# Experts stage: logits as eight more columns of Wo's matmuls, denominators inverted in a 128-partition layout, two decision groups, bf16 one-hot matrices

## The chip, the cores and the metric

One core of a Trainium2 chip. The metric is the device time of the whole program in microseconds, the median of the runs shown; each profile is of one execution more.

## What is computed

Two transformer layers with modulation, for 2048 tokens of 512 features. Layer 0 is attention and then a top-1 mixture of eight experts; layer 1 is a state-space block and a small block-diagonal MLP. The change lies in layer 0's second half, called experts here:

```
x = x + ga * (softmax-weighted values / denominators) @ Wo.T     (the end of attention)
h = layernorm(x) * (1 + cb) + sb
logits = h @ gate_w.T + gate_b;  selected = argmax(logits)
x = x + gb * (h @ expert_w[selected].T + expert_b[selected])
```

## The kernel before

`experts()` (lines 807 to 1372) holds 16 tiles of 128 tokens (TT), four to a chunk of 512 columns (PER, NCH). One list of instructions per engine is written by hand, and semaphores alone order them. All that follows is in the order of those lists.

**Start.** Attention has left numerators (`scratch.num`, 64 rows of 2048) and denominators (`scratch.den`, 8 rows) in memory. SP loads the numerators, Wo, a turned Wo, small constants and then the eight expert matrices of 1 MB (lines 945 to 957). ACT issues two loads of the denominators, each row repeated for the eight values of its head, so that they lie like the numerators, 64x2048 (L1119). PE spreads the gates over all partitions as rows (L997), takes the mean of the gate weights (L1004), the contribution of the shift to the logits (L1009), the product of the centred gate weights with x (L1015, four chunks, 32 rows each for four feature blocks, summed later by a matrix called collect) and Wo times the gate weights (L1020). ACT copies the product to SBUF as `xw` (L1125). DVE multiplies Wo by the gate row (L1200), then for each chunk inverts the 64x512 denominators (L1209); it multiplies chunk 0 itself (L1212), GpSimd the other three (L975).

**Loop over 16 tiles.** PE: Wo's matmul of a tile, 512 columns (L1050), then two matmuls of 8 columns that give its logits, one with `xw` and collect, one with Wo times the gate weights (L1051, L1052). A matmul in f32 is two passes in the trace. Three banks take Wo's results (A_BANKS). DVE: the residual, x plus that bank (L1218), statistics (L1222, L1226) and the inverse deviation (L1232, L1234). ACT: the square root (L1129) and, two tiles at a time, the normalised h (L1133), which it stores by chunks (L1136). The logits aren't of the normalised h: since the layer norm is linear but for its mean and deviation, they are the product of x with centred weights, scaled later by the inverse deviation.

**Decisions.** For each chunk of four tiles, `decide` (L1247 to L1254, eight steps of DVE, each waits for the one before) scales the logits, finds the largest and writes a one-hot matrix, `onehot`. PE counts by matmuls with a triangle and a matrix of ones (L1036, L1038, L1039, all f32), and `put` (L1264 to L1274) turns the counts into each token's rank with its expert, the number of full tiles before it, its row in its tile, and a matrix `at_row`. Decisions 0 to 2 and placements 0 and 1 stand in the loop of DVE, between tiles; the rest comes after the last tile.

**Tail.** DVE works out how many tiles of 128 each expert fills (L1299 to L1303), each token's tile, and the matrices (L1307 to L1310) with which PE (L1064) finds the source token of every slot in 23 tiles (TILES). GpSimd then issues indirect loads of h by these sources (L981). From then on PE turns each tile (L1079), multiplies it with its expert's matrix (L1099), and in between adds the experts' biases in four groups of four tiles (L1085 before tile 0, L1071 after tiles 0, 1, 2), turned by the one-hot rows from L1060. After the last tile the results are gathered back (L989), added and normalised, and the state space begins.

Of the kernel before, what the change touches and what calls it, by code (L numbers as in the profile page):

```python
# [17 lines left out]
F32 = mybir.dt.float32  # L18
BF16 = mybir.dt.bfloat16
# [787 lines left out]
def experts(nc, d, g, scratch):  # L807
# [9 lines left out]
    A_BANKS = 3  # L817
# [4 lines left out]
    PICK = 8  # L822
    TEMPER = float((HEADS * E) ** -0.5)
    with ExitStack() as ctx:
        sb, sem = sb_alloc(ctx, nc), sem_alloc(ctx, nc, "moe")
        wo = sb("moe_wo", [AC, D])
        wos = wo
# [4 lines left out]
        wow = sb("moe_wo_logits", [AC, EXPERTS])  # L832
        collect = sb("moe_collect", [P, EXPERTS])
# [6 lines left out]
        order = sb("moe_order", [P, 2, P])  # L840
        iota = sb("moe_iota", [P, EXPERTS])
        filled = sb("moe_filled", [P, NCH + 1, EXPERTS])
# [22 lines left out]
        onehot = sb("moe_onehot", [P, TT, 32])  # L865
        whole = sb("moe_whole", [P, EXPERTS, TT])
# [9 lines left out]
        above = sb("moe_above", [P, TT, TT])  # L876
        full = sb("moe_full", [P, TT])
        within = sb("moe_within", [P, TT])
# [7 lines left out]
        xw = srt  # L886
# [3 lines left out]
        ps_rows = [psum[:, b, :] for b in (0, 1)]  # L890
        ps_a = [psum[:, b, :] for b in range(A_BANKS)]
        ps_x = [psum[:, b, :] for b in (4, 5, 6, 7)]
        ps_gate = [psum[:, b, 0:PER * EXPERTS].rearrange("p (t e) -> p t e", e=EXPERTS) for b in (4, 5, 6, 7)]
        ps_pos = psum[:, 3, 0:(PER + 1) * EXPERTS].rearrange("p (t e) -> p t e", e=EXPERTS)
        ps_source = psum[:, 2, 0:TILES * 2]
        ps_mean, ps_c, ps_wow = (psum[:, b, 0:EXPERTS] for b in (3, 2, 3))
        ps_turn = psum[:, 4, :].rearrange("p (n t) -> p n t", n=NCH)
# [4 lines left out]
        logit_in, wo_in, count_in, experts_in = (sem(n) for n in ("logit_in", "wo_in", "count_in", "experts_in"))  # L902
        att_in = [sem("att_first_in"), sem("att_rest_in")]
        rows_mm, rows_out, gated, pool_set, den_done, first_ready, rest_ready = (sem(n) for n in (
            "rows_mm rows_out gated pool_set den_done first_ready rest_ready").split())
        wg_step, setup_mm, setup_out, x_mm, xw_out = (sem(n) for n in "wg_step setup_mm setup_out x_mm xw_out".split())
        WG_SCALED, WG_CENTRED, WG_GATED = 1, 2, 3
        MEAN_MM, C_MM, WOW_MM = 1, 2, 3
        PAD_SET, ONES_SET, HOTS_SET = 1, 2, 3
        att_mm, x1_done, stat_done, var_done, sd_done, rstd_done, shift_done, h_done, gate_mm = (sem(n) for n in (  # L910
            "att_mm x1_done stat_done var_done sd_done rstd_done shift_done h_done gate_mm").split())
        empty_set, pick, chosen_done, pos_mm, pos_step, ranked, place_step, found = (sem(n) for n in (
            "empty_set pick chosen_done pos_mm pos_step ranked place_step found").split())
# [12 lines left out]
        COUNTS = ((order[:], "order"), (iota[:], "iota"), (across[:], "across"), (row[:], "row"), (starts[:], "starts"), (tiles[:], "tiles"))  # L926
# [15 lines left out]
        def _(sp):  # L942
            for b in range(2):
                part = slice(b * HALF, (b + 1) * HALF)
                sp.dma_start(att[0:HEADS * E, part], scratch.num[:, part]).then_inc(att_in[b], 16)
                if b == 0:
                    sp.dma_start(wo[:], d["wo"]).then_inc(wo_in, 16)
                    sp.dma_start(wot[:], d["wot"].rearrange("(k p) c -> p k c", p=P)).then_inc(wo_in, 16)
# [44 lines left out]
        def _(pe):  # L993
# [34 lines left out]
            def positions(i):  # L1028

                pe.wait_ge(chosen_done, i + 1)  # L1030
                if i >= 1:
                    pe.wait_ge(ranked, i)
# [1287 lines left out]
```

## Time and profile before

| | us |
|---|---|
| median of 3 runs | 1777.32 |
| lowest, highest | 1776.28, 1777.55 |
| the profiled execution | 1780.89 |
| its span in the trace | 1779.1 |
| experts, before the first gather | 498.56 to 583.07 |
| busy in the span: PE, DVE, ACT, POOL | 1490.2, 1322.9, 1134.0, 924.0 |
| mean granted clock of TensorE | 0.874 |

The span is the profiled execution without what lies around it. A busy share is an average over stages with different bounds, so the stage of the change is read by its own stretches and in order of time. The granted clock is in parts of 2.4 GHz: 0.50 is the level of 1.2 GHz, 1.00 that of 2.4 GHz. An idle time in brackets is that of the engine just before, with what ended it.

### The profile page before, as it was taken

The page shows a single profiled execution, that of the slowest core. Times are in us where ns is not written, and L with a number is a line of the kernel's source. Part 1 is how long each engine was busy: PE and PEld are TensorE (multiplying, and loading weights), DVE is VectorE, ACT ScalarE, POOL GpSimd, SP SyncE. Part 2 cuts the span into 40 slices and gives each one's busy share as a digit, 9 for nine tenths or more (in the row PEclk, how much of TensorE's full clock was granted, in tenths as well). Part 3 has the DMA queues.
Part 4 walks back from the last instruction along what each step waited for, and adds up shares of the span by engine and source line. Part 5 has one row for each costly group of instructions (what it writes and reads, how often), then busy time and mean ns, then how long its engine had stood idle before and what let it go on. Part 6 is the DMA issues. An engine that isn't in the chain of part 4 may idle for free. (4 is left out here: it accounts for less than half of the span.)

```text
span 1779.1 us, 26522 instructions
## 1 busy us (share of the span) xinstructions
PE 1490.2 (84%) x9052; PEld 815.1 (46%) x9052; DVE 1322.9 (74%) x2126; ACT 1134.0 (64%) x2277; POOL 924.0 (52%) x603
## 2 busy tenths in 40 slices
PE   5888999999978895678688898998989888755668
PEld 2441222222246443556365575665657566422432
DVE  3339999999056414107999999999999999999232
ACT  2323777777922233347788878878887887855138
POOL 0000000001010223326999999999999999999303
PEclk9875999999965897699799899999999999866689
DMA  6411112221072345823354554555554554644112
GB/s 247 160 43 42 28 32 81 79 81 59 3 231 95 101 137 206 290 69 87 96 137 114 132 136 118 129 122 118 135 130 119 125 125 108 137 101 112 68 51 95
DMA packets 154386, 199.10 MB, mean 112 GB/s; under 512 B 17567, under 2 KB 124999, under 8 KB 152716
## 3 DMA queue, kind: packets, MB, share of 16 engines
q1 hardware_dynamic: 142252, 163.81, 34.3%
q0 software_dynamic: 5168, 18.63, 3.2%
q10 hardware_dynamic: 6832, 14.96, 2.3%
q8 instruction: 72, 1.18, 0.3%
q14 instruction: 62, 0.51, 0.1%
HBM read 151.08 MB, written 46.28 MB: 111 GB/s over the span
## 5 line engine op out<-in xcount | busy, mean ns | idle before, releaser
L2040 DVE TENSOR_TENSOR_SCAN shared<-ssm_psum,ssm_state,shared 128x256 f32<-128x256 f32 x1024 | 674.9, 722 | 20.7 <-ACT ssm_state L1927 12.2
L1940 ACT ACTIVATE ssm_psum<-shared,ssm_a 128x256 f32<-128x256 f32 x1024 | 443.6, 468 | 157.7 <-DVE shared L2040 151.3
L1662 POOL TENSOR_TENSOR shared<-shared,ssm_bc 128x1024 f32<-128x1024 f32 x256 | 509.3, 2000 | 35.4 <-DVE shared L2040 16.0
L734 ACT ACTIVATE att_probs<-att_psum 128x1024 f32<-128x1024 f32 x256 | 248.3, 1021 | 75.2 <-PE att_psum L661 72.6
L1639 POOL TENSOR_TENSOR shared<-shared,ssm_bc 128x1024 f32<-128x1024 f32 x144 | 287.9, 1999 | 12.2 <-DMA shared<-drive_rows 12.2
L775 DVE TENSOR_REDUCE att_rowmax<-att_psum 128x1 f32<-128x512 f32 x448 | 277.5, 681 | 3.3 <-PE att_psum L634 1.5
L1765 PE MATMUL ssm_psum<-shared,ssm_select 128*32 128x256 f32 x2048 | 170.4, 423 | 93.9 <-POOL shared L1662 93.3
L603 POOL COPY att_v<-v_tokens 128x128 f32<-128x128 f32 x8 | 2.3, 292 | 298.8 <-ACT att_out L728 298.8
L634 PE MATMUL att_psum<-att_k,att_q 32*128 32x512 bf16 x448 | 138.0, 398 | 9.9 <-DVE att_rowmax L775 7.3
L1700 PE MATMUL ssm_psum<-ssm_h,late_weights 128*128 128x256 f32 x512 | 133.0, 421 | 9.3 <-ACT shared L1900 5.4
L673 PE MATMUL att_psum<-att_probs,att_v 128*32 128x512 f32 x1024 | 137.2, 608 | 0.6 <-ACT att_probs L734 0.6
L661 PE MATMUL att_psum<-att_q,att_k 32*128 32x512 bf16 (+2 forms) x1344 | 136.7, 385 | 0.0
L2025 DVE TENSOR_TENSOR shared<-shared,ssm_psum 128x1024 f32<-128x1024 f32 x112 | 133.4, 1191 | 3.6 <-DMA shared<-drive_rows 3.6
L1751 PE MATMUL ssm_psum<-shared,late_weights 128*128 128x256 f32 x512 | 123.3, 396 | 7.9 <-ACT ssm_xout L1913 7.3
L1765 PEld LDWEIGHTS ssm_psum<-shared,ssm_select 128*32 128x32 f32 x2048 | 46.7, 112 | 180.0 <-POOL shared L1662 100.9
L1700 PEld LDWEIGHTS ssm_psum<-ssm_h,late_weights 128*128 128x128 f32 x512 | 107.0, 213 | 37.5 <-issue 13.1
L1743 PE MATMUL ssm_psum<-ssm_h,late_weights 128*128 128x256 f32 x512 | 123.6, 397 | 0.0
L1709 PE MATMUL ssm_psum<-ssm_upre,late_weights 128*128 128x256 f32 x512 | 117.2, 381 | 0.6 <-ACT late_turned L1846 0.5
L1751 PEld LDWEIGHTS ssm_psum<-shared,late_weights 128*128 128x128 f32 x512 | 99.2, 198 | 30.9 <-ACT ssm_xout L1913 9.7
L1743 PEld LDWEIGHTS ssm_psum<-ssm_h,late_weights 128*128 128x128 f32 x512 | 99.4, 198 | 23.0 <-issue 8.9
L1709 PEld LDWEIGHTS ssm_psum<-ssm_upre,late_weights 128*128 128x128 f32 x512 | 95.6, 189 | 19.8 <-issue 4.5
L661 PEld LDWEIGHTS att_psum<-att_q,att_k 18*128 18x128 bf16 (+2 forms) x1344 | 47.1, 93 | 115.5 <-ACT att_probs L734 89.8
(261 smaller groups left out, 1822.3 us busy)
## 6 DMA issues: line engine op xcount, KB each, us to landing
shared<-drive_rows SPq DMA_DIRECT2D x256, 256.0 KB, 4.5
qkv_wmod<-in_wmod SPq DMA_DIRECT2D x8, 1536.0 KB, 12.3
shared<-in_x SPq DMA_DIRECT2D x8, 1024.0 KB, 5.1
late_weights<-in_we SPq DMA_DIRECT2D x8, 1024.0 KB, 13.4
ssm_bc<-bc_rows SPq DMA_DIRECT2D x32, 256.0 KB, 5.2
drive_rows<-ssm_delta SPq DMA_DIRECT2D x64, 128.0 KB, 1.7
drive_rows<-ssm_du SPq DMA_DIRECT2D x64, 128.0 KB, 1.8
sorted_results<-moe_y ACTq DMA_DIRECT2D x23, 256.0 KB, 2.0
```

The lines of the kernel that those rows point to most:

```text
L661: last = nc.tensor.matmul(ps_s[half][:, j, :], kst[rows, s, a // 2, kt * P:(kt + 1) * P], qst[rows, s, a, :], start=(a == 0), stop=(a == P ...
L734: nc.scalar.activation(probs[:, u % RING, :].rearrange("p (j t) -> p j t", j=2), ps_s[u % 2], ACT.Exp).then_inc(exp_done, 1)
L775: nc.vector.tensor_reduce(rowmax[:, at:at + 1], ps_m[n % MB], AX.X, ALU.max).then_inc(max_done, 1)
L1639: nc.gpsimd.tensor_tensor(drive(Q), rep[:, s % 2, 1], bc[:, c % 2, 0, gr, :].unsqueeze(1).to_broadcast([P, J, SW]), ALU.mult).then_inc(poo ...
L1662: nc.gpsimd.tensor_tensor(read(Q), drive(Q), bc[:, c % 2, 1, gr, :].unsqueeze(1).to_broadcast([P, J, SW]), ALU.mult).then_inc(read_done, 1)
L1700: last = nc.tensor.matmul(halves("proj", c, pair)[:, i], win[:, k, m:m + P], h[:, c % 2, k, :], start=(k == 0), stop=(k == KT - 1))
L1709: last = nc.tensor.matmul(halves("conv", c, pair)[:, i], conv[:, 2 * pair + i, k, :], upre[:, pair % 2, i, k:k + SW], start=(k == 0), stop ...
L1743: last = nc.tensor.matmul(halves("gate", c, pair)[:, i], win[:, k, m:m + P], h[:, c % 2, k, :], start=(k == 0), stop=(k == KT - 1))
L1751: nc.tensor.matmul(bank("out", c, m)[:, 0:SW], wout[:, t, m * P:(m + 1) * P], gate[:, c % 2, t, :], start=(t == 0), stop=False)
L1765: last = nc.tensor.matmul(ps_y[t % 2][32 * j:32 * j + 32, :], select[:], read(Q)[:, j, :], start=(gr == 0), stop=False)
L1940: nc.scalar.activation(ps_decay[n % HALF_BANKS][:, i], rep[:, s % 2, 0, j, :], ACT.Exp, scale=amat[:, t, gr, j:j + 1]).then_inc(decay_done, 1)
L2040: nc.vector.tensor_tensor_scan(drive(Q)[:, j, :], ps_decay[(2 * Q + j // 2) % HALF_BANKS][:, j % 2], drive(Q)[:, j, :], state[:, t, gr, j: ...
```

## The change

The logits no longer have matmuls of their own. `att`, the left operand of Wo's matmul, grows from 65 to 104 rows: rows 96 to 103 hold the product of x with the centred gate weights (summed over the features by PE, copied by ACT and brought there by four DMAs from SP), rows 65 to 95 are zero. Wo grows by eight columns, which hold Wo times the gate weights and, in rows 96 to 103, an identity. The 520 columns are computed as two matmuls of 260 in two neighbouring banks; three such pairs replace the three banks. ACT copies the eight logit columns to SBUF and gives the pair free together with DVE.

The denominators are loaded once as 128 partitions x (8 heads x 16 tokens), inverted there, stored to memory and only then loaded repeated. DVE multiplies all four chunks, three of them in its loop. There are two groups of decisions, 12 tiles and 4; the first stands in the loop after tile 14's statistics, both placements after the loop. One-hot, triangle, ones and the identity that turns the one-hot rows are bf16. The number of full tiles comes from one addition that rounds to a multiple of 128 by a large constant instead of a comparison and a sum. The spreading of GATE_B, its copy and the bias product (now GpSimd's) move behind the loop; the first bias group moves behind tile 0. SP's expert weights come behind the four DMAs, which wait for the copy.

```diff
-    A_BANKS = 3
+    AR = 96 + EXPERTS
+    WIDE = D + EXPERTS
+    CUT = WIDE // 2
+    A_SLOTS = 3
+    GROUPS = ((0, 12), (12, TT))
+    TO_TILES = 3.0 * float(P << 22)
-        order = sb("moe_order", [P, 2, P])
+        order = sb("moe_order", [P, 2, P], BF16)
+        identity = sb("moe_identity", [P, P], BF16)
-        att = sb("moe_att", [AC, T])
+        att = sb("moe_att", [AR, T])
+        sums = sb("moe_sums", [P, HEADS, T // P])
-        onehot = sb("moe_onehot", [P, TT, 32])
+        onehot = sb("moe_onehot", [P, TT, 32], BF16)
+        ps_a = [flat[:, 2 * s * W + W - CUT:2 * s * W + W - CUT + WIDE] for s in range(A_SLOTS)]
```

On SP, behind the constants:

```diff
+            sp.wait_ge(xw_out, 1)
+            sp.wait_ge(pool_set, ONES_SET)
+            for i in range(NCH):
+                sp.dma_start(att[AR - EXPERTS:AR, i * W:(i + 1) * W], xw[32 * i:32 * i + EXPERTS, :]).then_inc(xw_in, 16)
+            sp.dma_start(be[:], d["be"]).then_inc(be_in, 16)
```

On GpSimd:

```diff
+            nc.gpsimd.memset(att[HEADS * E:AR - EXPERTS, :], 0.0).then_inc(pool_set, 1)
-            for i in range(1, NCH):
-                sl = slice(i * W, (i + 1) * W)
-                pool.wait_ge(den_done, i + 1)
-                nc.gpsimd.tensor_tensor(att[0:HEADS * E, sl], att[0:HEADS * E, sl], den[0:HEADS * E, sl], ALU.mult).then_inc(rest_ready, 1)
+            pool.wait_ge(rows_out, len(ROW))
+            pool.wait_ge(be_in, 16)
+            nc.gpsimd.tensor_tensor(bes[:], be[:], rows[:, ROW[GATE_B]], ALU.mult).then_inc(pool_set, 1)
```

On PE:

```diff
+            for k in range(KT):
+                for i in range(NCH):
+                    last = nc.tensor.matmul(ps_x[32 * i:32 * (i + 1), :], wc[:, k, :], xt[:, k, i * W:(i + 1) * W], start=(k == 0), stop=(k == KT - 1))
+            last.then_inc(setup_mm, 1)
+            pe.wait_ge(gated, 2)
+            pe.wait_ge(xw_in, 16 * NCH)
...
             for n in range(TT):
+                if n % PER == 0:
+                    pe.wait_ge(att_ready, n // PER + 1)
+                if n >= A_SLOTS:
+                    pe.wait_ge(x1_done, n - A_SLOTS + 1)
+                    pe.wait_ge(gate_out, n - A_SLOTS + 1)
-                nc.tensor.matmul(ps_a[n % A_BANKS], att[:, n * P:(n + 1) * P], wos[:], start=True, stop=True).then_inc(att_mm, 1)
-                nc.tensor.matmul(ps_gate[n // PER][:, n % PER, :], xw[:, n // PER, n % PER * P:(n % PER + 1) * P], collect[:], start=True, stop=False)
-                nc.tensor.matmul(ps_gate[n // PER][:, n % PER, :], att[:, n * P:(n + 1) * P], wow[:], start=False, stop=True).then_inc(gate_mm, 1)
+                a = ps_a[n % A_SLOTS]
+                nc.tensor.matmul(a[:, 0:CUT], att[:, n * P:(n + 1) * P], wo[:, 0:CUT], start=True, stop=True)
+                nc.tensor.matmul(a[:, CUT:WIDE], att[:, n * P:(n + 1) * P], wo[:, CUT:WIDE], start=True, stop=True).then_inc(att_mm, 1)
+                if n == 2:
+                    for k in range(KT):
+                        last = nc.tensor.matmul(ps_c, g.mod[:, 0, SHIFT_B, k:k + 1].to_broadcast([P, P]), wg[:, k, :], start=(k == 0), stop=(k == KT - 1))
+                    last.then_inc(setup_mm, 1)
+            positions(0)
+            pe.wait_ge(x1_done, TT)
+            pe.wait_ge(gate_out, TT)
+            spread_row(1, GATE_B)
+            positions(1)
```

On ACT:

```diff
+            act.dma_start(sums[:], scratch.den.rearrange("h (p b) -> p h b", p=P)).then_inc(sums_in, 16)
+            act.wait_ge(rows_mm, 1)
+            nc.scalar.copy(rows[:, 0], ps_rows[0]).then_inc(rows_out, 1)
+            act.wait_ge(sums_done, 1)
+            act.dma_start(scratch.rec.rearrange("h (p b) -> p h b", p=P), sums[:]).then_inc(sums_out, 16)
+            act.wait_ge(sums_out, 16)
-                act.dma_start(den[0:HEADS * E, part], scratch.den[:, part].unsqueeze(1).to_broadcast([HEADS, E, HALF])).then_inc(att_in[b], 16)
+                act.dma_start(den[0:HEADS * E, part], scratch.rec[:, part].unsqueeze(1).to_broadcast([HEADS, E, HALF])).then_inc(att_in[b], 16)
+            act.wait_ge(setup_mm, X_MM)
+            nc.scalar.copy(xw, ps_x).then_inc(xw_out, 1)
+            def logits(t):
+                act.wait_ge(x1_done, t + 1)
+                nc.scalar.copy(logit[:, t], ps_a[t % A_SLOTS][:, D:WIDE]).then_inc(gate_out, 1)
             for n in range(0, TT + 2, 2):
                 if n < TT:
+                    logits(n)
+                    logits(n + 1)
```

On DVE:

```diff
+            nc.vector.reciprocal(sums[:], sums[:]).then_inc(sums_done, 1)
-            for n in range(TT + 6):
+            for n in range(TT + 4):
...
+                if n % PER == 1 and n // PER + 1 < NCH:
+                    ready(n // PER + 1)
+                if n == GROUPS[0][1] + 2:
+                    decide(0)
+            put(0)
+            decide(1)
+            put(1)
...
-                step(nc.vector.tensor_tensor(above[:, sl], rank[:, sl].unsqueeze(2).to_broadcast(spread), starts[:].unsqueeze(1).to_broadcast(spread),
-                                             ALU.is_ge), pos_step, n + 5)
-                step(nc.vector.tensor_reduce(full[:, sl], above[:, sl], AX.X, ALU.add), pos_step, n + 6)
+                step(nc.vector.tensor_scalar(full[:, sl], rank[:, sl], 0.5 - P / 2, TO_TILES, ALU.add, ALU.add), pos_step, n + 5)
```

`ready(i)` waits for the numerators and the repeated inverses of its half and multiplies chunk i; it is called for chunk 0 before the loop. `positions(i)` is PE's counting for group i.

## Rows read from the trace of the kernel before

**Rows 1.** Stretches: us, busy PE, PEld, DVE, ACT, POOL, granted clock, DMA share, GB/s
```profile
512.00:514.00 2.00, 0.60 (x12) 0.50 (x8) 1.37 (x2) 1.87 (x2) 0.00 (x0) 1.00 1.05 397
527.00:566.00 39.00, 38.57 (x102) 25.04 (x102) 28.70 (x94) 10.52 (x19) 0.79 (x1) 0.50 0.27 102
720.00:1660.00 940.00, 776.62 (x4614) 526.42 (x4615) 830.97 (x1247) 708.04 (x1711) 848.32 (x514) 0.90 0.50 121
```

**Rows 2.** Timeline of the start; start us, us, engine, line, operation, count [idle before]
```profile
505.48 6.54 PE L1015 MATMUL moe_psum<-shared,moe_wg_centred 128*32 128x512 f32 x32
...
516.70 9.76 DVE L1209 RECIPROCAL moe_den<-moe_den 64x512 f32<-64x512 f32 x3
...
517.02 2.04 PE L1050 MATMUL moe_psum<-moe_wo,moe_att 65*128 65x512 f32 x2 [4.43 <-DVE moe_att L1212]
...
526.38 0.62 DVE L1218 TENSOR_TENSOR shared<-shared,moe_psum 128x512 f32<-128x512 f32 x1
```

**Rows 3.** Timeline of the loop over token tiles, PE, DVE and ACT
```profile
527.64 0.67 DVE L1218 TENSOR_TENSOR shared<-shared,moe_psum 128x512 f32<-128x512 f32 x1
...
528.96 0.67 DVE L1218 TENSOR_TENSOR shared<-shared,moe_psum 128x512 f32<-128x512 f32 x1
...
529.64 2.06 PE L1050 MATMUL moe_psum<-moe_wo,moe_att 65*128 65x512 f32 x2
...
530.86 0.68 DVE L1218 TENSOR_TENSOR shared<-shared,moe_psum 128x512 f32<-128x512 f32 x1
...
531.49 0.43 PE L1051 MATMUL moe_psum<-moe_collect,moe_sorted 128*128 128x8 f32 x2
...
531.77 0.57 PE L1052 MATMUL moe_psum<-moe_wo_logits,moe_att 65*128 65x8 f32 x2
...
532.20 2.06 PE L1050 MATMUL moe_psum<-moe_wo,moe_att 65*128 65x512 f32 x2
532.40 0.67 DVE L1218 TENSOR_TENSOR shared<-shared,moe_psum 128x512 f32<-128x512 f32 x1
...
533.39 1.50 ACT L1133 ACTIVATE shared<-shared,moe_shift,moe_rstd 128x512 f32<-128x512 f32 x2
...
566.44 0.68 DVE L1218 TENSOR_TENSOR shared<-shared,moe_psum 128x512 f32<-128x512 f32 x1
```

**Rows 4.** Timeline of the tail, up to the first gather
```profile
569.38 0.16 DVE L1264 TENSOR_TENSOR moe_filled<-moe_filled,moe_psum 128x8 f32<-128x8 f32 x1 [0.37 <-PE moe_psum L1039]
...
576.01 0.16 DVE L1264 TENSOR_TENSOR moe_filled<-moe_filled,moe_psum 128x8 f32<-128x8 f32 x1 [2.85 <-PE moe_psum L1039]
...
578.07 0.28 DVE L1299 TENSOR_TENSOR moe_whole<-moe_filled,moe_starts 128x128 f32<-128x128 f32 x1
...
581.50 0.79 PE L1064 MATMUL moe_psum<-moe_token,moe_at_row 128*128 128x46 bf16 x16 [3.66 <-DVE moe_token L1310]
...
583.07 1.00 POOL L981 DMA_INDIRECT moe_sorted<-tokens_normalised,moe_source_int  x1 [55.27 <-DVE moe_source_int L1317]
```

**Rows 5.** DMA issues: KB each, median us from issue to landing
```profile
late_weights<-in_we SPq DMA_DIRECT2D x8, 1024.0 KB, 13.4
...
mod_rows<-att_modcols POOLq DMA_DIRECT2D x1, 8.0 KB, 2.2
```

**Rows 6.** Timeline of SP's queue and of the wait for the turned Wo
```profile
499.74 0.42 SPq L948 DMA_DIRECT2D moe_wo_turned<-in_wot  x1
...
506.99 14.90 SPq L957 DMA_DIRECT2D late_weights<-in_we  x8
...
509.13 0.69 DVE L1200 SCALAR_TENSOR_TENSOR moe_wo<-moe_wo,moe_rows 65x512 f32<-65x512 f32 x1 [6.48 <-DMA moe_wo_turned<-in_wot]
```

**Rows 7.** Groups of instructions by form, experts
```profile
L1274 DVE TENSOR_TENSOR moe_at_row<-moe_across,moe_within 128x512 bf16<-128x512 f32 x4 | 2.8, 692 | 0.1
...
L1299 DVE TENSOR_TENSOR moe_whole<-moe_filled,moe_starts 128x128 f32<-128x128 f32 x1 | 0.3, 283 | 0.0
```

**Rows 8.** Timeline of the expert tiles, PE, one bias group
```profile
600.01 1.14 PE L1071 MATMUL moe_psum<-moe_be,moe_den 32*128 32x512 f32 x8
```

More of the change, by code:

```diff
@@ L1039, in positions @@
-                nc.tensor.matmul(ps_pos[:, 1:PER, :], order[:, 0], hot(slice(1, PER)), start=False, stop=True).then_inc(pos_mm, 1)
+                    pe.wait_ge(pos_step, 6 * i)
+                pe.wait_ge(count_in, 16 * len(COUNTS))
+                a, b = GROUPS[i]
+                for t in range(a, b):
+                    nc.tensor.matmul(ps_pos[:, t - a + 1:b - a + 1, :], order[:, 1], onehot[:, t:t + 1, 0:EXPERTS].to_broadcast([P, b - t, EXPERTS]),
+                                     start=(t == a), stop=False)
@@ L1080, in turn @@
                 last.then_inc(st_mm, 1)
-            pe.wait_ge(turned_out, 1)
-            pe.wait_ge(gated, 2)
-            for r in range(NCH):
-                last = nc.tensor.matmul(ps_bias[r], turned[32 * r:32 * (r + 1), 0, :], bes[32 * r:32 * (r + 1), :], start=True, stop=True)
-            last.then_inc(bias_mm, 1)
             pe.wait_ge(found, OWNER)
@@ L1101, in _ @@
                 last.then_inc(y_mm, 1)
-                if j + 1 < NCH:
-                    bias(j + 1)
+                if j < NCH:
+                    bias(j)
             pe.wait_ge(y_done, TILES)
@@ L1309, in _ @@
             nc.vector.tensor_scalar(token[:, :, :, 0], at_tile[:], row[:, 0:1], None, ALU.mult).then_inc(place_step, 1)
             nc.vector.tensor_tensor(token[:, :, :, 1], at_tile[:], starts[:].unsqueeze(2).to_broadcast(to_tile), ALU.mult).then_inc(found, 1)
-            step(nc.vector.tensor_tensor(past[:], ends[:].unsqueeze(1).to_broadcast(wide), tiles[:].unsqueeze(2).to_broadcast(wide), ALU.is_le), place_step, 10)
-            step(nc.vector.tensor_reduce(owner[:], past[:], AX.X, ALU.add), place_step, 11)
@@ L1313, in _ @@
-            step(nc.vector.tensor_scalar(owner[:], owner[:], float(EXPERTS - 1), None, ALU.min), place_step, 12)
+            step(nc.vector.tensor_tensor(past[:], ends[:].unsqueeze(1).to_broadcast(wide), tiles[:].unsqueeze(2).to_broadcast(wide), ALU.is_le), place_step, 11)
+            step(nc.vector.tensor_reduce(owner[:], past[:], AX.X, ALU.add), place_step, 12)
+            step(nc.vector.tensor_scalar(owner[:], owner[:], float(EXPERTS - 1), None, ALU.min), place_step, 13)
             nc.vector.tensor_copy(owner_int[:], owner[:]).then_inc(found, 1)
@@ L2300, in layouts @@
         "perm": np.ascontiguousarray(a["L1_ffn_perm"].reshape(KT, P).T).view(np.uint32),
-        "ident": np.eye(P, dtype=f), "group": group, "collect": np.tile(np.eye(32, EXPERTS, dtype=f), (KT, 1)),
-        "order": order, "across": every(range(-P, 0)), "row": np.arange(P, dtype=f)[:, None].copy(), "iota": every(range(EXPERTS)), "starts": every(range(0, T, P)),
-        "tiles": every(range(T // P + EXPERTS - 1)),
+        "ident": np.eye(P, dtype=f), "group": group, "identity": np.eye(P).astype(bf), "unit": np.ones((P, EXPERTS), f),
+        "order": order.astype(bf), "across": every(range(0, -P, -1)), "row": np.arange(P, dtype=f)[:, None].copy(), "iota": every(range(EXPERTS)), "starts": every(range(0, T, P)),
+        "tiles": every(range(0, T + (EXPERTS - 1) * P, P)),
     }
```

209 lines of the change are left out of this document (84 added, 125 removed).

## The prediction

> **What bounds the kernel now.** The chain that ended last follows only the final 6% of the span, so it says nothing of the experts. I read the stretches first [rows 1], then the order of time on PE, DVE and ACT between 498 and 606 us. The stage is serial: nothing of the gather can start before GpSimd's first indirect load, and what follows hangs on that load one after another (gather, 23 tiles, second gather, state space). So the question is how much earlier that load comes.
>
> Three stretches lead up to it. *Start:* PE has its first Wo tile under way at 517.02, but DVE goes into three reciprocals at 516.70 that take 9.76 us, so the first residual runs only at 526.38 [rows 2]. PE fills its three banks and stands. *Loop:* residuals run from 526.38 to 566.44 [rows 2, 3], 40.06 us for 15 steps. Between 527 and 566 PE is busy 38.57 of 39 us at a granted clock of 0.50 (1.2 GHz), DVE 28.70 [rows 1]. One tile costs PE 2.56 us: 1.85 for Wo's two passes, 0.71 for the four 8-column passes of the logits, the last two of them 0.43 [rows 3]. DVE needs 1.32 for an even tile and 1.54 for an odd one, 1.43 on average [rows 3]. PE is the bound except while a decision (1.7 us) and a placement (2.06) hold DVE. *Tail:* 566.44 to 583.07 is 16.63 us: 2.94 to the third placement, 6.63 for it and the last decision with PE's counting behind it, 2.06 for the last placement, 5.00 for the tile tables up to the load [rows 4].
>
> **The change, part by part.**
>
> *Start.* The reciprocals of 64x512 go (3.25 us each); one of 128x128 comes. Cost per column 3.25/512, so 0.8 us. In exchange the numbers make two more trips through memory: 1024 runs of 64 bytes in, as many out, then the old broadcast load. No row shows such a transfer. Nearest from below: 512 runs of 16 bytes on quiet queues land in 2.2 us [rows 5]. From above: the turned Wo, 512 runs of 260 bytes amid the other constants, was issued at 499.74 and ended DVE's wait at 509.13, 9.4 us [rows 6]. Several such constants still go out beside the new trips, fewer beside the second; I take 6 and 5. Then: in at 504.6, inverted 505.4, issued and landed 511.0, two broadcast issues on ACT's queue to 512.4. The copy of the 8 logit rows stands behind that wait in ACT's queue. PE's centred matmuls (6.54 us, [rows 2]) now come after one 1.7 us group and one row group and are ready near 509.3, so ACT is what is late. Copy 0.6 (as DVE's pass over such a tile), four issues of 0.42 [rows 3, 6], landing 2.2: 516.9. The broadcast lands beside it and its product (0.7) hides. First Wo tile at 516.9, first residual 2.06 later: **519.0, 7.4 us earlier.** With both trips at 2.3 the centred matmuls bind and it is 516; with both at 9.4 it is 526.5.
>
> SP is held too: the expert weights are queued behind the four strips and the wait for them. They were issued from 506.99 for 14.9 us [rows 6]; now from about 518, so 11 us later. They are needed at 561 or later, 43 us after; from 518 on, 14.9 of issue and a landing of 13.4 [rows 5] end at 546. Hidden; 15 us of cover are left. If that cover were gone, every microsecond past it would be paid in full.
>
> *Loop.* Per tile PE now has four passes of 260 columns, 1040 against 1024: 1.85 x 1040/1024 = 1.88 at the half clock at most, 1.73 if the weight loads hide under the next passes; 0.71 go. At the full clock it is under 0.95, and DVE's 1.43 binds. So the clock decides between DVE and PE. The old loop kept 0.50 throughout; the centred matmuls, which stream 512 columns without small ones between, were followed by 1.00 [rows 1, 2]. The new loop streams like those, and the state-space stage keeps 0.90 with PE not full [rows 1]. I take the half clock for the first tiles, the full one later. DVE-bound: 15 x 1.43 = 21.5; three products moved from GpSimd into DVE's loop, 0.62 each, 1.9; the group decision of 12 tiles before the last residual: eight steps, six of them on 96 columns, each somewhat under the 0.283 of 128 columns [rows 7], with gaps 2.2. Sum 25.6, plus 2 for the first tiles, in which the shift matmuls (eight short passes, 1.7) also stand between the third and fourth tile. **27.5: last residual at 546.5.** All at the half clock: four starts ahead, 14 x 1.73 + 1.7 + 1.3 + 2.2 = 29.5. Nothing lost at the start: 25.6.
>
> The logits' copy on ACT frees a bank. It can stand behind two passes of normalisation: 0.2 + 0.3 + 1.50 [rows 3] + 0.2, then a tile on PE 2.06 and the residual 0.6, 4.9 us for three tiles, 1.63 a tile at the half clock and 1.35 at the full. Just covered; no cover is left.
>
> *Tail.* Up to the first placement 2.65, as before up to the third (2.94) without its wait for PE. That placement covers 12 tiles: three steps of 0.3, two of 0.2, and the row matrix, 0.692 for 4 tiles [rows 7], 1.85 for 12: 3.1. Decision of 4 tiles, one step less: 1.5. PE's counting: six bf16 passes against 12 f32 ones. Sixteen bf16 passes of 46 columns took 0.79 [rows 4], 0.05 each; I take 0.9 with latency and the hand-over, bounds 0.5 and the 2.8 that f32 took. Last placement 2.06 - 0.3 = 1.75. Tables 5.00 - 0.1 = 4.9: two wide steps of 0.3 become short ones of 0.2, and one short step more of 0.2 comes. Sum 2.65 + 3.1 + 1.5 + 0.9 + 1.75 + 4.9 = 14.8 against 16.63. The GATE_B row, its copy and the bias product run beside this on PE, ACT and GpSimd, which wait for DVE here; without that cover they would be 2 + 0.6 + 1.3. **Load at 546.5 + 14.8 = 561.3, 21.8 us earlier.**
>
> *After the load.* The first bias group was in the gather's wait; now it follows tile 0, one more group of 1.14 us at the full clock [rows 8] in a PE-bound loop: 1.2 back. The rest is the same code. **Sum: 20.6 us faster.** Against its own 1780.9 us the profiled execution would give 1760.3; it is 3.6 above the median of the runs in the table, so the median goes from 1777.3 to **1756.7**.
>
> **A rule weighed.** The old loop had a full PE for 39 us and the clock stayed at 0.50 [rows 1]. The Trainium skill, "TensorE: Matmul & The Clock Gate", Part 1, says the default is the throttled rate and sustained activity releases it. By that sentence alone the old loop should have run at the full rate; the trace does not agree for a loop with many 8-column passes. By the page the new loop is fast and the median 1756.7, as I forecast; by the 0.50 of the old row it is slow, 1758.7, the first rival.
>
> The Trainium skill, "DMA: Bandwidth & Descriptors", section Why small descriptors are slow, speaks against the 64-byte runs: a fixed overhead per packet plus 32 bytes of metadata per operation. No run here shows that overhead by itself; by the page they cost more than their bytes, which is the side of the upper bound.
>
> **Rivals.**
> 1. *The loop stays at the half clock.* For: 0.50 over the whole old loop. Against: the small passes are gone. 29.5 instead of 27.5 us: 1758.7. Chance 0.2.
> 2. *The two trips take as long as the turned Wo.* For: they go beside those constants. 526.5 instead of 519.0: 1764.2. Chance 0.1.
> 3. *ACT's copy binds the ring*, a wait in the place of the one removed. For: 1.63 beside 1.73 leaves nothing. If each pair of tiles waited 1 us more, 7 us: 1763.7. Chance 0.05.
> 4. *Slower:* a 64-byte run costs an engine far more than any row shows. Each trip is 64 runs an engine. It turns slower when both together pass 11 + 20.6 = 31.6 us, 0.25 us a run; at 20 us a trip, 1785.7. Against: 16-byte runs land 512 at a time in 2.2 us. Chance 0.02.
> 5. *Nothing arrives:* the 20 us are given back behind the load, by expert weights landing late. The weights would have to land some 36 us later than I reckon, 15 to use up the cover and 21 to cost as much: 1777. Chance 0.02.
>
> The forecast has 0.61; its own ends are 516 at the start, 25.6 in the loop, 1 us in the tail: 1751 to 1760. The range reaches over the first three rivals to **1751 to 1764**. The first expert tile's eight wide passes cost some 3.7 us more at the half clock than at the full, by the 1.85 for two [rows 3]; where the clock rises there can move either end by 1.5. A measurement of this kernel can tell about 0.2%, 3.5 us. Faster 0.96, same 0.02, slower 0.02.
>
> **What would show it.** Right: one reciprocal of about 0.8 us; first residual between 516 and 522; residual to residual 1.4 to 1.75 us; a granted clock above 0.50 within the loop; DVE idle little in it; six short passes in under 1 us before the second placement; the load near 561; expert tiles of 3.9 us with four bias groups among them. Wrong: DVE or PE waiting for the DMA of the inverses past 522; 0.50 up to the last tile; PE waiting for ACT in the loop; PE waiting for expert weights after the gather; a state-space stage longer than before by more than 2 us.

## The result and the profile after

Four runs of the changed kernel gave 1753.52 to 1760.61 us, median 1755.57, against 1776.8 for the kernel before on the same chip: ratio 0.988, interval 0.9866 to 0.9895. On another chip, five more runs gave a median of 1753.59 against 1778.33, ratio 0.9873 (0.9855 to 0.9892). The forecast was 1756.7. Single runs far off all others (4165.87 us of small passes, 6316.19 of inverses alone, 4505.62 of the kernel before beside them) were in a slow state and are left out of every median and ratio here.

The profiled execution took 1760.61 us, span 1757.9, against 1779.1. Its experts' stage began at 500.83 instead of 498.56, which is attention's doing and no part of the change. So I read everything from the stage's own start: the first load of SP and ACT. Four sections add up to the span:

```
us                                     before    after   difference
start of the stage                     498.56   500.83    +2.27
stage start to GpSimd's first gather    84.51    62.55   -21.96
first gather to the second             104.11   104.57    +0.46
second gather to the end              1091.92  1089.95    -1.97
```

The first and last sections hold no changed work and vary by as much between executions (the first was 498.07 to 502.51 us and the last 1085.80 to 1091.92 over all fourteen profiles of this document). The change is in the two in the middle: 21.5 us.

The stretches after, loop and tail, then the second expert tile on, and the state space (us, busy PE, PEld, DVE, ACT, POOL, granted clock, DMA share, GB/s):

```profile
521.18:548.15 26.97, 19.57 (x68) 14.41 (x67) 24.82 (x68) 13.42 (x35) 0.00 (x0) 0.81 0.96 362
548.15:563.38 15.23, 4.57 (x60) 3.73 (x60) 13.13 (x48) 4.45 (x8) 1.26 (x1) 0.50 0.37 139
575.60:655.00 79.40, 79.40 (x263) 38.20 (x261) 23.07 (x35) 30.05 (x80) 16.05 (x17) 1.00 0.37 119
720.00:1660.00 940.00, 786.25 (x4661) 534.75 (x4659) 829.69 (x1240) 700.69 (x1699) 847.38 (x510) 0.90 0.47 115
```

Where [rows 1] had PE full, DVE with pauses and a clock of 0.50, the first line has DVE at 24.82 of 26.97 us, PE at 19.57 and a clock of 0.81. The bound of the loop has changed engine. From the second expert tile on PE is full at a clock of 1.00, and the state space has 0.90 as before.

The start, from its timeline (start us, us, engine, line, operation, count, idle before and what ended it):

```profile
500.83 0.40 ACTq L1122 DMA_DIRECT2D moe_sums<-att_den  x1
...
505.83 0.95 DVE L1216 RECIPROCAL moe_sums<-moe_sums 128x128 f32<-128x128 f32 x1 [2.29 <-DMA moe_sums<-att_den]
...
506.81 0.39 ACTq L1126 DMA_DIRECT2D att_den_inv<-moe_sums  x1
...
510.68 1.32 ACTq L1130 DMA_DIRECT2D moe_den<-att_den_inv  x2
512.03 0.58 ACT L1132 COPY moe_sorted<-moe_psum 128x512 f32<-128x512 f32 x1 [6.48 <-issue]
512.64 2.78 SPq L960 DMA_DIRECT2D moe_att<-moe_sorted  x4
515.13 0.68 DVE L1225 TENSOR_TENSOR moe_att<-moe_att,moe_den 64x512 f32<-64x512 f32 x1 [5.83 <-DMA moe_den<-att_den_inv]
...
519.00 1.20 PE L1050 MATMUL moe_psum<-moe_wo,moe_att 104*128 104x260 f32 x2 [8.76 <-DMA moe_att<-moe_sorted]
...
521.18 0.69 DVE L1235 TENSOR_TENSOR shared<-shared,moe_psum 128x512 f32<-128x512 f32 x1 [5.29 <-PE moe_psum L1051]
```

The three reciprocals of 9.76 us [rows 2], and one more ahead of them, have become one of 0.95. PE's first tile waits for the last of the four small DMAs. It comes hardly earlier than before (18.17 us after the stage's start, before 18.46), but its residual follows 2.18 us later, not 9.36.

The loop, from its timeline:

```profile
527.43 0.60 PE L1051 MATMUL moe_psum<-moe_wo,moe_att 104*128 104x260 f32 x2
527.86 0.67 DVE L1235 TENSOR_TENSOR shared<-shared,moe_psum 128x512 f32<-128x512 f32 x1
...
529.17 0.67 DVE L1235 TENSOR_TENSOR shared<-shared,moe_psum 128x512 f32<-128x512 f32 x1
...
530.55 0.68 PE L1050 MATMUL moe_psum<-moe_wo,moe_att 104*128 104x260 f32 x2 [1.65 <-ACT moe_logit L1137]
...
535.53 1.07 PE L1051 MATMUL moe_psum<-moe_wo,moe_att 104*128 104x260 f32 x2
...
536.64 0.69 DVE L1235 TENSOR_TENSOR shared<-shared,moe_psum 128x512 f32<-128x512 f32 x1 [1.11 <-PE moe_psum L1051]
```

The same two passes took 0.60 us at 527 and 1.07 at 535: the granted clock rose to 1.00 at about 525, fell back to 0.50 from 531 to 538 and rose again. PE waits four times for ACT's copy of the logits, 4.7 us in all. DVE waits for PE three times after the first residual, 1.5 us together: 0.25 before the second tile, when the clock was still 0.50, 1.11 at the end of the fall, and 0.16.

The tail, from its timeline:

```profile
546.04 0.15 DVE L1264 TENSOR_TENSOR moe_logit_bias<-moe_bg,moe_psum 128x8 f32<-128x8 f32 x1
...
548.15 0.68 DVE L1235 TENSOR_TENSOR shared<-shared,moe_psum 128x512 f32<-128x512 f32 x1
548.29 0.72 PE L1038 MATMUL moe_psum<-moe_onehot,moe_order 128*128 128x96 bf16 x12 [2.85 <-DVE moe_onehot L1273]
...
550.63 0.17 DVE L1283 TENSOR_TENSOR moe_filled<-moe_filled,moe_psum 128x8 f32<-128x8 f32 x1
...
551.98 1.76 DVE L1290 TENSOR_TENSOR moe_at_row<-moe_across,moe_within 128x1536 bf16<-128x1536 f32 x1
...
553.66 0.18 DVE L1267 TENSOR_TENSOR moe_logit<-moe_logit,moe_rstd 128x32 f32<-128x32 f32 x1
...
554.24 1.26 POOL L984 TENSOR_TENSOR moe_be<-moe_be,moe_rows 128x512 f32<-128x512 f32 x1 [48.91 <-ACT moe_rows L1153]
554.33 1.22 DVE L1270 TENSOR_TENSOR moe_logit<-moe_logit,moe_top 128x32 f32<-128x32 f32 x1
...
556.65 0.16 DVE L1283 TENSOR_TENSOR moe_filled<-moe_filled,moe_psum 128x8 f32<-128x8 f32 x1 [0.43 <-PE moe_psum L1041]
...
558.41 0.17 DVE L1313 TENSOR_SCALAR moe_padded<-moe_filled 128x8 f32<-128x8 f32 x1
...
563.38 1.00 POOL L990 DMA_INDIRECT moe_sorted<-tokens_normalised,moe_source_int  x1 [7.88 <-DVE moe_result_int L1332]
```

DVE's wait of 2.85 us for the last counting [rows 4] is now 0.43. One line doesn't fit: DVE's L1270 on 32 columns took 1.22 us, its neighbours 0.19. GpSimd's bias product (L984) ran from 554.24 to 555.50, and L1270 ended at 555.55.

### The profile page after: what moved, and what is told of

It is laid out like the page before. It is cut to its first block and busy times, and to the rows that moved or that the text cites. A ratio compares the mean times of both kernels' runs of the same rounds, so it can differ in the third digit from the quotient of the medians.

```text
span 1757.9 us, 26360 instructions
## 1 busy us (share of the span) xinstructions
PE 1458.5 (83%) x8976; PEld 795.0 (45%) x8976; DVE 1307.6 (74%) x2088; ACT 1134.2 (65%) x2290; POOL 923.4 (53%) x602
## 6 DMA issues: line engine op xcount, KB each, us to landing
late_weights<-in_we SPq DMA_DIRECT2D x8, 1024.0 KB, 14.5
```

## The experiments

Where an experiment has one or a few runs, its median can't tell 1 us. So each is judged by the same places in its profile, in us from its own stage's start. One profile has a limit too: three moves and filled wait have the same code up to the first gather and reach it at 60.82 and 62.64 us, because the clock rose at different times in their loops.

```
kernel                  1st residual  last residual  1st gather  to the 2nd   median
before                         27.82          67.88       84.51      104.11  1777.3
inverses alone                 21.90          66.78       83.43      103.08  1778.8
after                          20.35          47.32       62.55      104.57  1755.6
after, again                   20.08          46.93       62.15      104.58  1753.6
old inverses                   25.77          51.24       66.47      105.99  1761.5
small passes                   20.50          61.79       77.02      105.99  1769.9
wide pass                      19.85          47.44       62.66      104.60  1757.1
f32 one-hot                    19.25          46.00       67.66      104.63  1761.8
four groups                    19.74          53.50       67.14      105.68  1761.5
bias first                     19.90          45.65       60.88      103.21  1753.0
copy earlier                   20.22          46.01       61.24      104.41  1756.0
strips first                   20.32          46.09       61.32      104.39  1758.4
three moves                    19.82          45.60       60.82      103.85  1753.4
filled wait                    19.61          47.42       62.64      108.98  1761.2
```

**1. Small passes put back** into the kernel after, two matmuls (four passes) a tile with results that nobody reads:

```diff
                 nc.tensor.matmul(a[:, CUT:WIDE], att[:, n * P:(n + 1) * P], wo[:, CUT:WIDE], start=True, stop=True).then_inc(att_mm, 1)
+                for _ in range(2):
+                    nc.tensor.matmul(ps_pos[:, 0, :], att[:, n * P:(n + 1) * P], wo[:, D:WIDE], start=True, stop=True)
```

> The changed kernel with two useless 8-column matmuls (four passes) after each tile's Wo matmuls, as many as the old loop had; their result is not used. Theory of the clock: small passes among the wide ones hold the granted clock at 0.50, PE takes about 2.6 us a tile and bounds the loop: 76 us from stage start to first gather instead of 62.6, total about 1770. Rival: the clock rises all the same, PE needs under 1.4 us a tile, DVE bounds: 63 to 65 us.

Measured: 1769.88 us, ratio to before 0.9951 (0.993 to 0.9972). Its loop:

```profile
520.56:561.85 41.29, 41.05 (x131) 35.17 (x131) 25.80 (x68) 13.84 (x35) 0.00 (x0) 0.50 0.64 236
```

The clock never rose: 0.50 over the whole loop, PE full, 2.75 us a tile, and 14.5 of the 22 us in front of the gather are gone. The theory held (76 us to the first gather expected, 77.02 measured).

**2. One wide pass instead**, of about the same cost on PE at the half clock:

```diff
+                nc.tensor.matmul(psum[:, 6, 0:CUT], att[:, n * P:(n + 1) * P], wo[:, 0:CUT], start=True, stop=True)
```

> The kernel after, with one further pass of 260 columns per tile, whose result nobody reads, in the place where the small-passes kernel had two of 8 columns. At half the clock a tile then costs TensorE 1.5 times 1.73, 2.6 us; with the small passes it was 41.29 over 15 steps, 2.75 us. So both kernels begin the loop with nearly the same load on TensorE and differ in the shape of the passes. Theory (the shape holds the clock down: short passes keep it at 0.50, wide ones let it rise): the granted clock rises within some microseconds of the first tile, the mean over the loop is 0.8 or more, a tile at the full clock costs 1.3 us and hides under VectorE's 1.43, the loop takes 26 to 29 us, the load comes 62.5 to 64.5 us after the stage's start, the time is 1755 to 1758 us. Rival (a loop in which TensorE is never idle stays at 0.50, whatever its passes): clock 0.50 throughout, loop 15 x 2.6 = 39 us, load at 75, time 1768 us.

Measured: 1757.05 us, ratio 0.9883 (0.9867 to 0.9899). Its loop:

```profile
519.58:547.17 27.59, 23.50 (x100) 19.01 (x99) 24.88 (x67) 13.33 (x35) 0.00 (x0) 0.93 0.96 363
```

Half as much work again for PE costs the loop 0.6 us, because the clock rose: from 4 us in it was 1.00. The two experiments begin with PE nearly equally loaded at the half clock (2.75 and 2.60 us a tile); they differ in the added passes, four of 8 columns or two of 260. So the small passes cost far more than their own time: they kept the loop at half the clock.

Is that more than one execution's chance? The moment of the rise does vary a lot. In the eleven profiles without small passes it came between 1 and 11 us after the first residual; in filled wait (experiment 10) PE was busy 12.37 of 12.40 us at 0.50 before it. But it came in all eleven, and in none of the three with small passes (small passes, the kernel before, inverses alone), whose loops last 40 to 45 us. The times agree: the runs of small passes took 1767.06 to 1772.13 us, those of wide pass 1754.59 to 1758.61. What it is in the small passes that holds the clock, their length, their number or the weight load that each brings, no run separates.

**3. The denominators' turn alone**, in the kernel before (four reciprocals of 64x512 out; one of 128x128, the store and the load of the inverses in):

```diff
+            act.dma_start(sums[:], scratch.den.rearrange("h (p b) -> p h b", p=P)).then_inc(sums_in, 16)
+            act.wait_ge(den_done, 1)
+            act.dma_start(scratch.rec.rearrange("h (p b) -> p h b", p=P), sums[:]).then_inc(sums_out, 16)
-                nc.vector.reciprocal(den[0:HEADS * E, sl], den[0:HEADS * E, sl]).then_inc(den_done, 1)
+            nc.vector.reciprocal(sums[:], sums[:]).then_inc(den_done, 1)
```

> The kernel before with the denominators' turn alone (loaded as 128 partitions, inverted once, stored, loaded repeated; GpSimd keeps three of the products). Read from the stage's first load to the first gather: 84.5 us before. My theory: the first residual comes some 10 us earlier (27.8 to about 17 us after the stage's start), but PE at 2.56 us a tile is what bounds the loop and had three tiles done in advance, so only 6 to 7 us arrive: 78 us, total about 1770. Rival: the removed DVE time arrives in full, 74 us. Rival: nothing arrives, since PE bounds, 84 us.

Measured: 1778.79 against 1777.66 us, ratio 1.0008 (0.9994 to 1.0023), no difference. Loop and tail:

```profile
520.33:565.21 44.88, 44.06 (x117) 28.46 (x117) 30.18 (x97) 10.53 (x19) 2.40 (x2) 0.50 0.45 165
565.21:581.86 16.65, 8.95 (x76) 7.84 (x80) 11.86 (x51) 3.70 (x6) 0.00 (x1) 0.50 0.34 126
```

The first residual came 5.9 us earlier and the loop became 4.8 us longer. I had expected the first gather at 78 us; it came at 83.43, by the rival that nothing arrives. The old loop is PE's, and PE's first tile was no earlier (19.75 us against 18.46). While DVE inverted, PE had been filling its three banks; that head start is lost when DVE is early. What went is PE's own wait for the first residual, 2.22 us before, and 1.3 us of that were spent again on the later first tile.

**4. The old inverses in the kernel after**, the same edit the other way round.

> The changed kernel with the four 64x512 reciprocals back on DVE and the direct broadcast load. Stage start to first gather: 62.6 us in the changed kernel. My theory: first Wo tile early enough, first residual behind the reciprocals at about 23.6 us instead of 20.4, three tiles in advance then: 65 to 66 us, 2.5 to 3.5 slower than the changed kernel. Rival: the loop is bound by DVE, so DVE's removed 12 us count in full: 72 us or more.

Measured: 1761.46 us, ratio 0.9903 (0.9876 to 0.993). First residual 5.4 us later, loop 1.5 us shorter (25.47), first gather 3.9 us later. So this part is worth about 4 us, and only once the loop is DVE's. Some of the 1.5 is not the edit's: this loop had no fall of the clock, which costs the kernel after 1.1 us (experiment 8).

**5. The counting in f32** (`order`, `identity`, `onehot` without BF16):

> The changed kernel with one-hot, triangle, ones and identity in f32. My theory: the counting of 12 tiles is 28 passes instead of 14 and no longer ends before DVE asks for it, and that of 4 tiles is 12 passes of 0.21 us at the half clock instead of 6 short ones; stage start to first gather 2.5 to 5.5 us longer than the 62.6. Rival: the counting is hidden by DVE's work, no difference over 0.5 us.

Measured: one run of 1761.79, against 1780.57 for the kernel before on that chip. Timeline:

```profile
546.97 5.29 PE L1038 MATMUL moe_psum<-moe_onehot,moe_order 128*128 128x96 f32 x24 [2.81 <-DVE moe_onehot L1273]
...
553.28 0.16 DVE L1283 TENSOR_TENSOR moe_filled<-moe_filled,moe_psum 128x8 f32<-128x8 f32 x1 [3.89 <-PE moe_psum L1041]
...
561.75 0.17 DVE L1283 TENSOR_TENSOR moe_filled<-moe_filled,moe_psum 128x8 f32<-128x8 f32 x1 [2.85 <-PE moe_psum L1041]
```

The tail took 21.66 instead of 15.23 us. DVE's first wait cost 3.9 and its second 2.4 more than with bf16. The count of a 12-tile group, 0.72 us in bf16, takes 5.29 in f32, and DVE's work covers only the start of it. The first gather came 5.1 us later than in the kernel after and not 6.4, since start and loop happened to be 1.3 us shorter in this execution.

**6. Four groups** instead of two, `GROUPS = ((0, 4), (4, 8), (8, 12), (12, TT))`, decisions and placements in the loop as before.

> The changed kernel with four groups of decisions as before, in the loop as before. My theory: DVE bounds the loop, and three groups of 4 tiles cost it about 4.8 us more than one of 12 (3 x 3.3 against 5.1): 67 us from stage start to first gather. Rival: DVE has room in the loop where PE is at the half clock, which hides most: 63 to 64 us.

Measured: one run of 1761.5. The loop took 33.76 us, 6.8 more, the tail 13.64, 1.6 less; DVE's busy time in the loop rose from 24.8 to 30.0 and the clock was 0.60. By the first gather two groups are worth 4.6 us, as forecast. DVE's own work is 5.2 of the 6.8; the rest goes with the clock, which rose late and fell again in this profile, and with it DVE's waits for PE (1.85 and 0.32 us).

**7. Three small moves**, each alone: the first bias group back into the wait for the gather; ACT's logits copy one tile further ahead; the copy of the 8 logit rows ahead of the broadcast loads.

```diff
+            bias(0)
             pe.wait_ge(found, OWNER)
...
+                    if n == 0:
+                        logits(0)
-                    logits(n)
                     logits(n + 1)
+                    if n + 2 < TT:
+                        logits(n + 2)
```

> The changed kernel with the first bias group back ahead of tile 0, in the gather's wait. My theory: first gather to second gather 104.6 us in the changed kernel becomes 103.4, since the group no longer stands in PE's loop. Rival: tile 0 meets the half clock longer or PE is not the bound there, 104.6 as it is.

> The changed kernel with each even tile's logits copied ahead of the square root and of the two normalisations on ACT, not behind them. PE's 4.7 us of waiting for ACT's copy should go. Theory 1: those waits also cost the clock in the loop and DVE some 1.5 us of waiting for PE; stage start to first gather 1 to 2 us shorter than 62.6. Theory 2: DVE bounds, PE's waits are its slack, and nothing changes within 0.4 us.

> The changed kernel with ACT copying the centred product and so SP sending the four strips ahead of ACT's wait for the inverses. My theory: the strips go out 2.5 us earlier and the first Wo tile starts 2.5 us earlier (15.6 us after the stage's start instead of 18.2), and all of it arrives: 60 us to the first gather. Rival: the landing is set by the load of the inverses beside it, which comes as late as before (product ready at 15.0 us), and the strips land late in any order; under 1 us arrives.

Measured, one run each: 1753.01, 1756.01 and 1758.35 us. Bias first: first to second gather 103.21 instead of 104.57, 1.4 us: 1.14 for the group, and a tile 0 that was 0.26 us shorter. Copy earlier: PE's waits for ACT fell from 4.7 to 3.0 us, and the first gather came at 61.24, no earlier than in the two kernels beside it that lack this edit (60.88, 61.32). Strips first: the copy ran at 511.19, 9.8 us into the stage instead of 11.2, the four DMAs were issued 1.4 us earlier, and PE's first tile came at 18.14 instead of 18.17. Their landing took 5.0 us from the last issue where it had taken 3.6, so the gain was lost between issue and landing.

All three had a loop of 25.75 to 25.79 us where the kernel after had 26.97, though bias first has the very same loop. That led to the next run.

**8. The kernel after once more.**

> The kernel after once more, unchanged, on the same chip as the next two, to compare them with it and to see a second profiled execution. In the first one the granted clock fell back to 0.50 between 531 and 537 us of the loop and the loop took 26.97 us; three kernels whose loop is the same up to that point took 25.75 to 25.79 at a mean clock of 0.96. Theory (the fall comes and goes by execution): the loop takes anything from 25.7 to 27.1 us here and the load comes 61.2 to 62.6 us after the stage's start. Rival (the fall belongs to this code): 26.9 to 27.0 again, with the clock at 0.50 for some 6 us. Time 1755.5, within 1.5.

Measured: 1753.59 us, ratio 0.9873. The loop took 26.85 us at a mean clock of 0.75:

```profile
518.15:545.00 26.85, 21.11 (x68) 15.60 (x67) 24.85 (x67) 13.42 (x35) 0.00 (x0) 0.75 0.97 364
```

So both profiles of this kernel, and the one of f32 one-hot (26.75 us, 0.76), show the fall of the clock in mid-loop, for 7 to 10 us, and so does four groups, for 16. Bias first, copy earlier, strips first and three moves don't (0.94 to 0.96), nor do old inverses, wide pass and filled wait. The fall costs 1.1 us: 26.75 to 26.97 us against 25.75 to 25.79. By the loop's code bias first should be with the former, by its profile it is with the latter. What sets it stays open.

**9. The three moves together.**

> The three small moves together: first bias group in the wait for the gather, logits' copy of the next pair one step earlier, copy of the 8 logit rows ahead of the broadcast loads. By their single profiles only the first gave anything of its own: load to second gather 103.21 against 104.57, 1.36 us. Theory: 1.4 us under the kernel after on the same chip (about 1754), with the loop at 25.7 to 27 us and its first Wo tile at 18.1 us. Rival (the earlier copies hold the clock up too, since TensorE no longer stands between two pairs): 2.6 us under it (about 1753), the loop always at 25.8.

Measured: 1753.38 us (four runs), ratio 0.9867 (0.9849 to 0.9885), beside 0.9873 (0.9855 to 0.9892) for the kernel after on that chip: no difference that the runs can tell. Its profile has the first gather 1.3 us earlier and the second 2.1. Tile 0 took 5.42 us here and 4.67 in bias first, since the clock rose later.

**10. The wait filled**: the three moves, and four more passes in PE's wait of 2.25 us for the gather.

```diff
+            for r in range(4):
+                nc.tensor.matmul(ps_y[1], turned[0:32, 0, :], bes[0:32, :], start=True, stop=True)
```

> The three moves and, behind the first bias group, four more passes with the same operands (32 rows deep, 512 columns) whose result nobody reads, in TensorE's wait of 2.25 us for the gather's first load. Theory (a busy TensorE ahead of the first expert tile lets the clock rise sooner): tile 0's eight matmuls take about 3.7 us instead of 4.67 and its turn 0.7 instead of 1.1, load to second gather 101.7 to 102.3 us, the time 1 to 1.5 us under the three moves alone. Rival: the passes run at half the clock into the landing of the load and push the first turn back by up to 1 us, tile 0 stays at 4.7, load to second gather 103.2 to 104.2.

Measured: 1761.17 us, ratio 0.9905 (0.989 to 0.992), slower than without them by 7.8. Timeline of PE:

```profile
560.99 2.09 PE L1080 MATMUL moe_psum<-moe_be,moe_den 32*128 32x512 f32 x8
562.86 7.03 PE L1097 MATMUL moe_psum<-moe_be,moe_den 32*128 32x512 f32 x8
569.82 1.97 PE L1088 MATMUL moe_psum<-ident,moe_sorted 128*128 128x128 f32 x8
572.62 6.02 PE L1107 MATMUL moe_psum<-late_weights,moe_ht 128*128 x8 [0.83 <-ACT moe_ht L1172]
```

I had sized the four matmuls by the bias group, 2.09 us for four. That group's lie on four different sets of 32 rows; mine all lay on the same one and took 7.03. They are also unlike in their target, one bank of PSUM instead of four, and no run separates the two; 7.03 us is the time of eight passes one behind another, 0.88 us each. The first turn ran 4.5 us later than in the three moves, by the distance from the gather's issue (3.50 us there, 7.98 here). First to second gather took 5.1 us more, outside both the theory and the rival. The profile has a further 2 us in the loop, which this edit doesn't touch:

```profile
518.81:546.62 27.81, 20.34 (x68) 15.36 (x67) 24.81 (x68) 13.55 (x35) 0.00 (x0) 0.81 0.90 336
```

Here the clock rose 11 us into the loop, against 3 in the three moves, with the same code up to there. Whether the other runs of this kernel had that too, one profile can't say; so 5.1 us is what the edit is shown to cost. The clock didn't rise early for the added passes either: from 560.3 to 577 PE had one pause of 0.83 us and was busy otherwise, at 0.50 all the time, and tile 0 took 6.02 us.

## Why the prediction was right, point by point

**The sum.** First gather forecast 21.8 us earlier, measured 21.96; after it 1.2 back, measured 0.46; together 20.6 against 21.5. The difference of the medians is 21.2 and 24.7 on the two chips. The terms are less even than the sum, and part of the match is luck.

**Start.** First residual forecast 20.44 us after the stage's start, measured 20.35. Two misses of about 2.5 us each cancelled, which is luck. The trips through memory took 5.0 and 3.9 us, with the issue, where I had 6 and 5: 2.65 us early at the copy, with the shorter issues counted. Then the four small DMAs cost 2.78 us to issue, where I had 1.68 from constants on SP, and 3.6 to land, where I had 2.2 from an idle queue. I had taken both values from the nearest rows, of other transfers at other times; no run shows whether the shape of these four or the traffic beside them made them slower. A 64-byte run was cheap: 1024 of them landed in 3.8 us.

The Trainium skill, "DMA: Bandwidth & Descriptors", section Why small descriptors are slow, names a fixed overhead for each packet and operation, and so spoke for the upper bound here. The trace agrees only in part: the 1024 runs of 64 bytes took more than the 2.2 us of [rows 5] and far less than the 9.4 of [rows 6].

What I had not seen is that the 7.4 us would not count in full. Experiments 3 and 4 price the early residual at 1.1 us in the old loop and 3.9 in the new one. The forecast stood because it counted the new loop from the first residual and bound it by DVE.

**Loop.** Forecast 27.5 us, measured 26.97 and 26.85, bound by DVE, with the clock rising after some tiles, as the step had it. That the small passes had held the clock down is shown by experiments 1 and 2. The steps of 1.32 and 1.54 us and the decision (2.11, forecast 2.2) are as taken. The 2 us for the first tiles were not: DVE waited only 0.25 us for PE there. What I had not expected, the fall in mid-loop, cost 1.1 us and filled most of that gap, so that the match of the loop is luck in this term. Without the fall the same steps took 25.75 us (bias first), which is the forecast's own lower end of 25.6. A first part at the half clock that costs what I took does occur: in four groups and filled wait, where the clock rose about 11 us in, DVE waited 1.85 and 0.32 us more.

The Trainium skill, "TensorE: Matmul & The Clock Gate", Part 1, says that activity releases the throttle. With the small passes a PE busy 41.05 of 41.29 us stayed at 0.50, with the wide one the clock was 1.00 from 4 us into the loop. The trace agrees for wide passes, after 1 to 11 us of the loop, and not for short ones; by that sentence alone the two would be alike.

**Tail.** Forecast 14.8 us, measured 15.23, by the forecast's terms: up to the placement 2.48 (2.65), placement 3.03 (3.1), decision 2.62 (1.5), counting 0.37 (0.9), last placement 1.76 (1.75), tables 4.97 (4.9). The decision is the miss, by 1.1 us; the counting, 0.5 under its forecast, gave half of that back. I had costed GpSimd's bias product at nothing, since it runs beside DVE. In each of the twelve profiles that have it there, one DVE instruction with two operands in SBUF lies beside it and ends with it: 1.22 us for L1270 here, and, where the product meets another point of DVE's list, 1.25 for L1267 in f32 one-hot and 0.93 for L1287 in four groups:

```profile
559.34 1.27 POOL L984 TENSOR_TENSOR moe_be<-moe_be,moe_rows 128x512 f32<-128x512 f32 x1 [55.10 <-ACT moe_rows L1155]
...
559.51 0.18 DVE L1286 TENSOR_TENSOR moe_logit<-moe_psum,moe_filled 128x32 f32<-128x32 f32 x1
559.72 0.93 DVE L1287 TENSOR_TENSOR moe_logit<-moe_logit,moe_onehot 128x32 f32<-128x32 f32 x1
```

The Trainium skill, "SBUF — State Buffer", section Who interferes with whom, says that GpSimd and a VectorE operation with two SBUF inputs lock each other out of a shared port pair. The trace agrees: L1286 above, with one of its inputs in PSUM, ran in 0.18 us beside the product, and L1270, with both in SBUF, took 1.03 us more than its neighbours. No run took the product away, so the cost is shown by coincidence in twelve profiles, not by an experiment.

**After the gather.** One more bias group costs 1.14 us, as taken; tile 0's matmuls took 4.93 us, where they had taken 5.66, because the clock rose sooner in them, after 2.5 us and not after 4.0. That is the 0.7 by which I was off, within the 1.5 I had allowed for it.

**Rivals.** The half clock to the end: no, but it is what happens when the small passes stay, at 14.5 us. Long trips: no, 5.0 and 3.9. ACT's copy binds: PE waits for it in the loop, which I had named as a sign of being wrong, but DVE hardly does, and moving the copy shows no gain (experiment 7). Slower through 64-byte runs: no. Nothing arrives: no, the expert weights' last issue ended near 531 and no tile waited for them.

## What to carry to other kernels

A very short matmul pass can cost more than its own time: look at the granted clock of the loop that it stands in before counting microseconds, and see whether its columns fit into a pass that runs anyway. The clock can differ between executions of the same code, so look at more than one profile before giving a microsecond to an edit. A faster start is worth only what the engine that bounds the following loop gains; ask which engine had been working ahead in the old wait. Work moved to an idle engine isn't always free: see whether an instruction of the critical engine stretches beside it.

## What the runs showed of the hardware

- Four passes of 8 columns beside four of 260 in each tile kept the granted clock at 0.50 for 41 us; with two further passes of 260 in their place it rose to 1.00 (mean 0.93).
- Without the short passes the clock rose between 1 and 11 us after the first residual. With the same code up to there it rose 3 us in once (three moves) and 11 us in once (filled wait), PE being busy 12.37 of the 12.40 us before.
- Four f32 matmuls of 32 rows by 512 columns took 2.09 us on four different sets of 32 rows (and into four banks) and 7.03 on the same one (and into one bank), both at half the clock.
- After a wait, tile 0 of the experts took 4.67, 4.84, 4.93, 5.42, 5.66 or 6.02 us for the same eight matmuls, by when in it the clock rose.
- In all twelve profiles with the product in the tail a DVE operation of 0.19 us (128x32, two operands in SBUF) stretched to 0.93 to 1.25 us beside a GpSimd product of 1.26 to 1.79 us.
